# First attention: probabilities times values from fp16 halves in three products instead of one fp32 product

## The reference, cut to what matters

```python
    def _L0_xattn_ref(hidden_states, cond, ...):
        ln_out = _ln(hidden_states, ln_w, ln_b)
        q = _ln(_fp8_linear_pertensor(ln_out, wq, wq_scale, q_in_scale).reshape(b, s, g, hpg, d), qln_w, qln_b)
        k = _ln(_fp8_linear_pertensor(ln_out, wk, wk_scale, k_in_scale).reshape(b, s, g, d), kln_w, kln_b)
        v = _fp8_linear_pertensor(ln_out, wv, wv_scale, v_in_scale).reshape(b, s, g, d)
        core = _gqa(q, k, v).reshape(b, s, nh * d)
        ...
        xout = _gqa(qx, kx, vx).reshape(b, s, nh * d)       # the same with keys and values of the context
        cat = jnp.concatenate([core, xout], axis=-1)
        catq = _div_clamp_fp8(cat, proj_smooth)
        return jnp.einsum('bsi,oi->bso', catq, wproj) * (proj_in_scale * proj_w_scale)

    def _gqa(q, k, v):
        p = jax.nn.softmax(jnp.einsum('bsghd,btgd->bghst', q, k) * scale, axis=-1)
        return jnp.einsum('bghst,btgd->bsghd', p, v)
```

## Time and profile before

| | us |
|---|---|
| three timed runs, median | 3048.16 (3046.93 to 3048.58) |
| the profiled execution, its own time | 3051.39 |
| span of its trace, first to last instruction | 3049.6 |
| PE busy in the span | 2834.9 (93%) |
| DVE busy | 1807.4 (59%) |
| ACT busy | 1703.4 (56%) |
| POOL busy | 1749.1 (57%) |

### The profile page before, as it was taken

How to read it: one execution, slowest core, us unless ns; L and a number is a source line. 1 busy time by engine, 2 the same in 40 slices (tenths; PEclk the granted TensorE clock), 3 DMA queues, 4 the chain that set the end, 5 groups by cost and what they waited for, 6 DMA issues and landing times. The chain is left out here.

```text
span 3049.6 us, 57678 instructions
## 1 busy us (share of the span) xinstructions
PE 2834.9 (93%) x16353; PEld 1636.1 (54%) x16354; DVE 1807.4 (59%) x5590; ACT 1703.4 (56%) x4562; POOL 1749.1 (57%) x2443
## 2 busy tenths in 40 slices
PE   4699999999999969999999999959999999985998
PEld 2366666666666644555555555424555555543664
DVE  4366666666666646433443444539989988863443
ACT  5578777787777742332332333427777777751332
POOL 6467777777777624544453544447677777731222
PEclk9899999999999989999999999979999999998999
DMA  7711121111211145544554454735665555557444
GB/s 244 257 43 50 56 80 59 49 49 56 80 59 49 46 142 166 158 136 138 161 154 135 139 159 136 215 76 114 122 137 132 118 131 129 127 108 292 83 81 68
DMA packets 467530, 360.90 MB, mean 118 GB/s; under 512 B 295521, under 2 KB 366305, under 8 KB 467425
## 3 DMA queue, kind: packets, MB, share of 16 engines
q1 hardware_dynamic: 404912, 282.85, 32.5%
q0 software_dynamic: 16496, 37.79, 6.2%
q10 hardware_dynamic: 46016, 38.99, 4.4%
HBM read 186.23 MB, written 110.39 MB: 97 GB/s over the span
## 5 line engine op out<-in xcount | busy, mean ns | idle before, releaser
L1393 POOL TENSOR_TENSOR e_st<-e_st,e_ws_tile 128x1024 f32<-128x1024 f32 x64 | 123.9, 1936 | 429.0 <-PE e_y L1149 417.3
L752 ACT ACTIVATE a_nrm<-a_mm,a_sc_t 128x128 f32<-128x128 f32 x768 | 290.9, 475 | 123.5 <-POOL a_sc_t L905 123.3
L603 DVE BATCH_NORM_STATS2 a_st<-a_mm 128x6 f32<-128x128 f32 x768 | 170.5, 284 | 290.5 <-PE a_mm L440 208.0
L439 PE MATMUL a_mm<-a_w_hi,a_xq_hi 128*128 128x512 f16 x768 | 296.9, 387 | 23.3 <-POOL a_xq_lo L887 15.1
L1187 ACT ACTIVATE e_hh<-e_ha 128x512 f16<-128x512 f32 x128 | 76.3, 596 | 413.3 <-PE e_ha L1134 412.0
L440 PE MATMUL a_mm<-a_w_hi,a_xq_lo 128*128 128x512 f16 x768 | 297.0, 387 | 0.0
L1282 DVE SCALAR_TENSOR_TENSOR e_hl<-e_ha,e_hh 128x512 f16<-128x512 f32 x128 | 88.4, 691 | 351.7 <-ACT e_hh L1187 351.3
L904 POOL TENSOR_TENSOR a_sc_t<-a_sc_t,a_mhalf 128x4 f32<-128x4 f32 x192 | 204.1, 1063 | 118.5 <-DVE a_sc_t L610 118.2
L1148 PE MATMUL e_y<-e_w2l,e_hh 128*128 128x512 f16 x640 | 242.6, 379 | 0.0
L1147 PE MATMUL e_y<-e_w2h,e_hh 128*128 128x512 f16 x640 | 242.6, 379 | 0.0
L1149 PE MATMUL e_y<-e_w2h,e_hl 128*128 128x512 f16 x640 | 242.6, 379 | 0.0
(11 more groups left out here) (366 smaller groups left out, 8221.4 us busy)
## 6 DMA issues: line engine op xcount, KB each, us to landing
e_st<-in_w SPq DMA_DIRECT2D x128, 512.0 KB, 4.1
disp<-a_empty SPq DMA_DIRECT2D x16, 2084.0 KB, 8.0
e_st<-in_w1b SPq DMA_DIRECT2D x32, 352.0 KB, 3.1
disp<-a_empty SPq DMA_DIRECT2D x4, 2605.0 KB, 21.5
e_xb<-disp SPq DMA_DIRECT2D x40, 260.5 KB, 4.3
e_xb<-disp ACTq DMA_DIRECT2D x40, 260.5 KB, 2.7
a_cx<-in_ctxT SPq DMA_DIRECT2D x32, 256.0 KB, 3.3
a_stage<-in_wprojT SPq DMA_DIRECT2D x16, 512.0 KB, 4.9
```

The costliest lines, as they stand in the source:

```text
L439: pe.matmul(out, xq_hi[:, n, c, :], w_hi[:, t, c, :], start=(c == 0), stop=False)
L752: ins = act.activation(nrm[:, n % 2, i * P:(i + 1) * P], src[:, i * P:(i + 1) * P], ACT.Identity, bias=sc_t[:, n % 2, 3, i:i + 1], scale=s ...
```

## The change

The values and the transposed probabilities are each stored as two fp16 tensors, a high half and a low half. ACT writes the high half (for the probabilities scaled by `PS` = 1024, which is taken out again in `rsm`); DVE reads the same PSUM bank again and subtracts the high half, in the new stages `p_low` (u + 4) and `v_low` (job + 2). `p_ok` and `v_ok` now count the low halves, and the new `p_hi` and `v_hi` the high ones. `pv` makes three fp16 products of 256 columns (high x high, low probabilities x high values, high probabilities x low values) in place of each fp32 one.

```diff
-        vt = s.sb("vt", [P, 4, DM], F32)
+        vt = [s.sb(f"v{n}", [P, 4, DM], F16) for n in ("h", "l")]
...
-        pT = s.sb("pT", [P, 2, DM], F32)
+        pT = [s.sb(f"p{n}", [P, 2, DM], F16) for n in ("h", "l")]
...
@@ pv
-                    mm = pe.matmul(OVB[:, i * 256:(i + 1) * 256], vt[:, KV_OF[a], g * P:(g + 1) * P],
-                                   pT[:, a % 2, i * 256:(i + 1) * 256], start=True, stop=True)
+                    for n, (vn_, pn) in enumerate(((0, 0), (0, 1), (1, 0))):
+                        mm = pe.matmul(OVB[:, i * 256:(i + 1) * 256], vt[vn_][:, KV_OF[a], g * P:(g + 1) * P],
+                                       pT[pn][:, a % 2, i * 256:(i + 1) * 256], start=(n == 0), stop=(n == 2))
...
-            ch.link(dve.tensor_scalar(rsm[:], rsm[:], QS, None, ALU.mult))
+            ch.link(dve.tensor_scalar(rsm[:], rsm[:], QS / PS, None, ALU.mult))
...
+            def p_low(b, a):
+                dve.wait_ge(sem["p_hi"], at(a, NA, b))
+                dve.scalar_tensor_tensor(out=pT[1][:, a % 2, :], in0=PTB[:], scalar=PS, in1=pT[0][:, a % 2, :],
+                                         op0=ALU.mult, op1=ALU.subtract).then_inc(sem["p_ok"], 1)
+
+            def v_low(b, t):
+                if t in v_no:
+                    col = 3 if "X" in JOBS[t] else 4
+                    dve.wait_ge(sem["v_hi"], at(v_no[t], NV, b))
+                    i = V_NAMES.index(JOBS[t])
+                    dve.scalar_tensor_tensor(out=vt[1][:, i, :], in0=MMB[BANK[t]][:], scalar=scal[:, col:col + 1],
+                                             in1=vt[0][:, i, :], op0=ALU.mult, op1=ALU.subtract)\
+                       .then_inc(sem["v_ok"], 1)
...
-            run_pipeline(dve, [("att", 2, row_scale), ("att", 1, smax), ("att", 6, o_quant), ("end", 10, final), ("end", 10, r_stats),
+            run_pipeline(dve, [("att", 2, row_scale), ("att", 1, smax), ("att", 4, p_low), ("job", 2, v_low), ("att", 6, o_quant), ("end", 10, final), ("end", 10, r_stats),
...
-                    act.activation(vt[:, i, :], src[:], ACT.Copy, scale=scal[:, col:col + 1])\
-                       .then_inc(sem["v_ok"], 1)
+                    act.activation(vt[0][:, i, :], src[:], ACT.Copy, scale=scal[:, col:col + 1])\
+                       .then_inc(sem["v_hi"], 1)
...
-                act.activation(pT[:, a % 2, :], PTB[:], ACT.Copy).then_inc(sem["p_ok"], 1)
+                act.activation(pT[0][:, a % 2, :], PTB[:], ACT.Copy, scale=PS).then_inc(sem["p_hi"], 1)
```

More of the change, by code:

```diff
@@ L272, in layer0_attention @@
             "x_in", "c_in", "x_stat", "x_scal", "x_norm", "x_tr", "x_t", "y_act", "y_pool", "xq", "xq_ok", "cx_hi", "cx_lo",
-            "mm", "stat", "scal", "norm", "v_ok", "qtr", "q_ok",
-            "score", "max", "exp", "rinv", "pnorm", "ptr", "p_ok", "pv", "oy", "cq", "proj",
+            "mm", "stat", "scal", "norm", "v_hi", "v_ok", "qtr", "q_ok",
+            "score", "max", "exp", "rinv", "pnorm", "ptr", "p_hi", "p_ok", "pv", "oy", "cq", "proj",
             "xres", "x1", "out", "filled", "disp_filled", "rconst", "r_stat", "r_scal", "r_norm", "r_tr", "r_t",
```

## The result

| | before | after |
|---|---|---|
| median, seven timed runs each | 3048.16 us (3046.88 to 3052.52) | 3058.62 us (3054.75 to 3062.06) |
| the profiled execution, its own time | 3051.39 | 3057.22 |
| from one `x_transpose` to the next, one batch | 63.40 | 64.34 |

The ratio is 1.0031, 95% interval 1.0019 to 1.0042: slower by 0.31%, some 10 us. The prediction was 3040 and its range 3029 to 3053, so sign and range are both missed.

The account below looks back on a forecast made before the run. PE was taken to bound the first attention, busy 927.3 of 934 us. The terms -25.4 + 13.5 + 2.1 + 1.5 + 0.5 = -7.8 us gave 3043.6 from the profiled 3051.39, or 3040 as median; range 3029 to 3053.

Parts of the forecast that it names:

- The product: On PE, six fp16 products in 0.655 us replace 0.87 us; 0.215 gained on each of 118, 25.4 us.
- DVE's load: Twelve low halves per batch at 0.69 us add 8.3 us on DVE, to 49.7 or 78% busy, hidden by busy time.
- Slot 2, `r_transpose`: PE waits there for `p_keep`, now also for the low half: 0.965 us per batch, 13.5 us in 14.
- Slot 9, r_pos: `p_transpose` on PE waits for a later r_pos from DVE: 0.15 us per batch, 2.1 us in 14.
- Ends: Low halves queued on DVE before the last batch's last product cost 1.5 us, the first batch 0.5.
- The V bank and the other banks: `project` wants a V job's bank at about 619, free at 617.7; this and the other users cost nothing.
- The rounding's long case: DVE's rounding after `o_quant` takes 1.30 us for one pass, not 0.43; bound 1.0 us per batch at slot 9's wait.
- DVE's queue falls behind: Rival, 28%: low halves wait for ACT, rounding runs long, r_pos comes 1.0 us late; 11.9 us more, 3052.
- The text's own test for being wrong: The prediction is wrong if PE waits in a third place in every batch, or a batch is over 63.4 us.

Follow-up runs that it names:

- e3: The changed kernel with `p_keep` ahead of `normalise` in ACT's order; 3026.97 us, ratio to before 0.9933.
- e5: The kernel before, fp32 product kept, with `p_low` and `v_low` added on DVE into tiles that nothing reads; 3072.53 us, ratio to before 1.0078.
- e7: The changed kernel without `v_low`, the values' low half left at zero, `p_low` kept; 3075.96 us, ratio to before 1.0098.
- e10: The changed kernel with only the `p_low` of slot 14 (attention 2) moved behind `o_quant` and its rounding on DVE; 3033.38 us, ratio to before 0.9958.

## Why the prediction was wrong

- *The product*, -25.4. Right. After, six records take 641.67 - 641.01 = 0.66 us (0.655 forecast), so no weight load of 0.10 is added to a product:

```profile
641.01 0.27 PE L492 MATMUL a_ovb<-a_ph,a_vh 128*128 128x256 f16 x1
...
641.67 0.38 PE L505 MATMUL a_prb<-a_wp,a_cq 128*128 128x512 f16 x1
```

- *DVE's load*, 8.3 us per batch at 0.69 each. Near: the low halves take 8.5, since `v_low` takes 0.74, and DVE is busy 8.9 more per batch.
- *Slot 2, `r_transpose`*, +13.5 from 0.965 per batch. Right in mechanism; PE's idle time there rose by 0.78, which is 10.9, 2.6 less than forecast. e3 shows what makes it: ACT's order.
- *Slot 9, r_pos*, +2.1. Not there: no such wait in any batch from 190 to 1110 us.
- *Ends*, +2.0. From the last `x_transpose` (991.19 before, 1002.03 after) to the last `out_project` 1.8 us are added, of which 0.9 are a batch's usual loss; at the third `x_transpose` (166.96 and 166.10) PE is 0.9 ahead. So about nothing.
- *The V bank and the other banks*, "all at nothing". This step failed. The text said that `project` wants a bank "three jobs later" and looked at a V job in slot 6. The walk covered slot 2 and slots 6 to 9 and left out slots 13 to 1, where QX3's bank has one slot less and DVE's `r_stats` and QX3's `stats` lead to it. The term put at nothing costs 1.62 per batch, 22.7 us. With -7.8 forecast that is +14.9; less 2.6 in slot 2, 2.1 in slot 9 and 2.0 of the ends, and with the 2.4 of `q_transpose`, which the sum hadn't either, +10.6. Measured are 12.6 at the end of the stage and 10.5 in the medians.
- *The rounding's long case* was named, with a bound of 1.0 per batch, for slot 6. There both passes take 0.43. It came in slot 14, in both passes, where the row of before had 0.43.
- *The rival "DVE's queue falls behind"* had the right sign and kind (28%): the low halves wait for ACT's high half, the rounding takes its long case, PE waits. It had the place wrong, and so the price: 11.9 against 22.7. The text's own test for being wrong, a third place of wait in every batch or a batch over 63.4, is what the profile of after shows.

The cause is shown and not only argued: the wait for QX3's bank comes with the low halves alone (e5), stays without those of the values (e7), and goes, with 23 us, when one low half changes places with its neighbour (e10). Read from the trace and not tested apart is how the late queue of slot 14 reaches the bank: how much of it the 1.4 us of longer rounding makes, and how much comes over POOL's wait for `r_stats`. Open is the second attention of e7.

## What to carry to other kernels

A buffer's slack is the time between the row that frees it and the row that uses it next, read for every use in the period, and not only where a wait is listed: this one had 0.15 us of slack and stood in no list. Look first for the uses that break the pattern, here what the `+ [1]` in the table of banks makes of jobs 13 and 15. And follow a late instruction to every engine that waits for it: here `r_stats` held up POOL, which had other work behind it. And where a new instruction waits for another engine, put it behind the work that is ready: the same twelve instructions cost 40 us more in one order of two queues than in the other.

## What the runs showed of the hardware

A rounding pass on DVE (`tensor_scalar`, 128x1024 of two bytes, in and out of SBUF) takes 0.43 us alone and 1.13 to 1.3 beside a GpSimd operation on 128x512. In the rows above the pass that starts at 645.45 ends at 646.58, 0.27 after GpSimd's operation (645.15 to 646.31), and the next at 647.77, 0.29 after GpSimd's (646.38 to 647.48): it looks held until the other is done, and not slowed by a share. The Trainium skill ("SBUF — State Buffer", Who interferes with whom) has this as a rule: a `tensor_scalar` of DVE can take the pair of ports that DVE shares with GpSimd, and then the second of the two to issue blocks until the first is done. The trace agrees for GpSimd's operations on 128x512. It does not for a narrow one. In the kernel before the pass at 638.68 starts while this operation on 128x4 runs, and takes 0.43 all the same:

```profile
637.98 1.17 POOL L904 TENSOR_TENSOR a_sc_t<-a_sc_t,a_mhalf 128x4 f32<-128x4 f32 x1 [0.58 <-DVE a_sc_t L610]
```

A pass beside an operation on 128x512 costs 0.7 us more. In slot 14 the rounding starts 1.5 us later than by the pace of before (645.45 for 638.68 + 5.27 = 643.95), and both passes then fall there.
